# The row-maximum pass of a windowed attention in tiles of 32 queries x 4 heads by 160 keys

## What is computed

```python
mask = (j <= i) & (j >= i - 128)
q = (x @ Wq.T + bq).reshape(B, 512, 16, 8)    # k and v alike
scores = einsum('bqhd,bkhd->bhqk', q, k) / sqrt(8)
scores = where(mask, scores, -10000.0)
attn = softmax(scores, axis=-1) + 1e-9
ctx = einsum('bhqk,bkhd->bqhd', attn, v).reshape(B, 512, 128)
return ctx @ Wo.T + bo
```

## Time and profile before

| | us |
|---|---|
| median of 3 runs | 1092.84 (1092.12 to 1097.75) |
| the profiled execution's span | 1090.0 |
| TensorE busy in it | 783.8 (72%) |
| VectorE | 704.6 (65%) |
| GpSimd | 573.2 (53%) |
| ScalarE | 410.4 (38%) |

### The profile page before, as it was taken

The page is one execution under the profiler, slowest core; times in us unless marked ns, Lnnn a source line. Parts: engine busy times, 40 slices in busy tenths (PEclk is TensorE's granted clock), DMA queues, the critical chain, the costliest instruction groups (busy, mean ns, idle before and its releaser), DMA issues.

```text
span 1090.0 us, 21702 instructions
## 1 busy us (share of the span) xinstructions
PE 783.8 (72%) x6716; PEld 547.0 (50%) x6716; DVE 704.6 (65%) x2608; ACT 410.4 (38%) x690; POOL 573.2 (53%) x633
## 2 busy tenths in 40 slices
PE   4811887886677879788897979877777666666671
PEld 3611676665555525445454544445346555455560
DVE  7687778753545597675768667586857953445444
ACT  1360254443332415353434434354425433333330
POOL 5591562756545014463646443366447666666661
PEclk9999957998888959896989898896556898889886
DMA  8110012232223201010111101001002111222214
GB/s 233 26 29 10 21 41 60 57 60 62 57 65 79 71 22 50 21 53 23 48 47 29 51 12 49 3 3 30 11 15 61 38 45 45 62 74 82 69 40 128
DMA packets 62750, 54.05 MB, mean 50 GB/s; under 512 B 9986, under 2 KB 55812, under 8 KB 62636
## 3 DMA queue, kind: packets, MB, share of 16 engines
q1 hardware_dynamic: 53108, 33.12, 10.4%
q0 software_dynamic: 9536, 19.55, 7.1%
...
## 4 chain that ended last, share of the span: by engine, by line
PE 41%; DVE 28%; issue 10%; another core or an unknown queue 5%; ACT 5%; DVEq 4%; POOL 4%; DMA 3%; SPq 0%; POOLq 0%; ACTq 0%
PE stbank L1124 6%; DVE sbank L838 4%; PE stbank L1111 3%; PE sbank L1182 3%; PE bank L1211 3%; DVE zr L597 3%; PE stbank L1113 3%; PE stbank L1196 3%; PE stbank L1125 2%; DVE gl L778 2%; PE stbank L1112 2%; DVE xs L794 2%; ACT pT L966 2%; PE bank L1245 2%
## 5 line engine op out<-in xcount | busy, mean ns | idle before, releaser
L475 POOL DMA_INDIRECT xg<-table,idx x156 | 159.0, 1019 | 139.6 <-PE sbank L1092 63.4
L917 ACT ACTIVATE g<-stbank 128x512 f32<-128x512 f32 x156 | 93.3, 598 | 326.2 <-PE stbank L1113 247.6
L1124 PE MATMUL stbank<-wff,gh 128*128 x624 | 141.2, 305 | 100.1 <-DVE ysb L768 59.1
L838 DVE CUSTOM_DVE_ANT_0 sbank<-sbank,mband 128x256 f32<-128x256 f32 x384 | 152.2, 454 | 40.4 <-PE sbank L1182 29.9
L541 POOL TENSOR_SCALAR_AFFINE_SELECT pT<-pT 128x512 f32<-128x512 f32 x128 | 82.0, 641 | 177.3 <-ACT pT L966 177.0
L1111 PE MATMUL stbank<-xT,wff 128*128 128x128 f16 x624 | 151.2, 248 | 18.9 <-issue 11.1
L966 ACT ACTIVATE pT<-stbank 128x1024 f32<-128x1024 f32 (+1 forms) x128 | 116.9, 914 | 125.5 <-PE stbank L1196 124.6
L768 DVE TENSOR_REDUCE ysb<-stbank 128x128 f32<-128x256 f32 x156 | 65.9, 422 | 151.4 <-remote 90.1
L1113 PE MATMUL stbank<-xT,wff 128*128 128x128 f16 x624 | 151.5, 248 | 0.0
L1112 PE MATMUL stbank<-xT,wff 128*128 128x128 f16 x624 | 148.8, 244 | 0.0
L1124 PEld LDWEIGHTS stbank<-wff,gh 128*128 128x128 f16 x624 | 67.0, 107 | 132.5 <-issue 114.2
...
...
## 6 DMA issues: line engine op xcount, KB each, us to landing
...
qz<-dumps SPq DMA_DIRECT2D x96, 32.0 KB
kst<-dumps SPq DMA_DIRECT2D x96, 32.0 KB
xg<-table,idx POOLq DMA_INDIRECT x156
...
```

The costliest lines, as they stand in the source:

```text
L475: g.indirect_dma_start(xg[:, i % G].rearrange("p a d -> p (a d)"), None, table[cc % 2], bass.IndirectOffsetOnAxis(ap=idx[:, cc % 2, t:t + ...
L838: ins = v.tensor_tensor_reduce(out=src, in0=src, in1=m[:], scale=1.0, scalar=-3e38, op0=ALU.add, op1=ALU.max, accum_out=mx[:, qt, 4 * s + ...
L1124: mm(o, gh[:, i % 3, P * f:P * f + P], whl, start=(f == 0), stop=False, skip_group_check=True)
```

## The change

The maximum pass is tiled in another way. The queries of a block are numbered 32 n + q, with n = 0 to 3. One matmul takes the 32 queries of one n for all four heads of the set (4 x 32 = 128 rows) against the 160 keys that they can see. Two such make a half unit (`QW` = 32, `KW` = 160). Only the first and the last 32 of the 160 keys need a mask, the same triangles for every n: a third matmul adds them, `head4` (four identities side by side) times `corners`. In the first block, keys before the sequence's start are filled by small matmuls against `masked`, and each half unit has five matmuls. VectorE then takes one plain maximum over 2 x 160 per half unit.

To let one matmul pick the queries of one n of all heads, `qz` is laid out as (set and block, head, q, n), n fastest, so the weights are read with a step of four elements. With it change: the order of features in Wq and Wk (`head_order`), the write order of `hi`, `lo` (four instructions each) and `mT`, the pieces in which the stacks are read back, the affine selects' patterns on GpSimd, whose columns are now (q, n), and the transposes of `cx`, which become fp32 matmuls with a permutation (`unorder`) that puts the queries back in order.

```diff
@@ -32,6 +32,8 @@
+QW = 32
+KW = P + QW
@@ -98,7 +100,8 @@
-        mband = sb("mband", [P, 256], F16); mlower = sb("mlower", [P, P], F16)
+        head4 = sb("head4", [P, 4, QW], F16); corners = sb("corners", [P, 2, QW], F16); masked = sb("masked", [P, 1], F16)
+        unorder = sb("unorder", [P, 4, QW])
@@ -132,6 +135,8 @@
+        qv = qz[:].rearrange("p u (s t) (g n) -> p u s t g n", s=SETS, g=4)
@@ -176,6 +181,10 @@
+        def ordered(a, i):
+            a = a[:, i, :]
+            return a.rearrange("p (t q n) -> p t n q", q=QW, n=4) if i == 0 else a.rearrange("p (t n q) -> p t n q", n=4, q=QW)
@@ -336,10 +345,12 @@
                 for m in (2 * (k - 2), 2 * (k - 2) + 1):
                     i, g, c = m // 12, m // 3 % 4, m % 3
                     part = ((0, 0, 1), (0, 1, 0))[i][c]
-                    src = dumps[par, 2 * i + part].rearrange("(g s j) n -> g j s n", g=4, s=SETS)[g]
+                    src = dumps[par, 2 * i + part].rearrange("(g j s) n -> g j (s n)", g=4, s=SETS)[g]
...
-                    dst = (qz[r:r + DK, slot].rearrange("p (s g) n -> p s g n", g=4)[:, :, g, :] if i == 0 else kst[r:r + DK, slot, :, :])
-                    sp.dma_start(dst, src).then_inc(s_stk[par], 16)
+                    if i == 0:
+                        sp.dma_start(qz[r:r + DK, slot, :, P * g:P * g + P], src.rearrange("j (r n) -> j r n", n=P)).then_inc(s_stk[par], 16)
+                    else:
+                        sp.dma_start(kst[r:r + DK, slot].rearrange("j s n -> j (s n)"), src).then_inc(s_stk[par], 16)
@@ -517,15 +530,16 @@
-            made(g.affine_select(out=mband[:], in_=mband[:], compare_op=ALU.is_ge, fill=MASKED, base=0,
-                                 pattern=[[1, 256]], channel_multiplier=-1))
-            made(g.affine_select(out=mlower[:], in_=mlower[:], compare_op=ALU.is_ge, fill=MASKED, base=0,
-                                 pattern=[[-1, P]], channel_multiplier=1))
+            made(g.affine_select(out=head4[0:QW], in_=head4[0:QW], compare_op=ALU.not_equal, fill=1.0, base=0,
+                                 pattern=[[0, 4], [1, QW]], channel_multiplier=-1))
+            made(g.affine_select(out=corners[0:QW, 0, :], in_=corners[0:QW, 0, :], compare_op=ALU.is_ge, fill=MASKED, base=0,
+                                 pattern=[[1, QW]], channel_multiplier=-1))
+            made(g.affine_select(out=corners[0:QW, 1, :], in_=corners[0:QW, 1, :], compare_op=ALU.is_ge, fill=MASKED, base=0,
+                                 pattern=[[-1, QW]], channel_multiplier=1))
+            made(g.affine_select(out=unorder[:], in_=unorder[:], compare_op=ALU.not_equal, fill=1.0, base=0,
+                                 pattern=[[-1, 4], [-4, QW]], channel_multiplier=1))
...
-            pool.wait_ge(s_chain, made_n[0])
-            made(g.affine_select(out=mband[:], in_=mband[:], compare_op=ALU.is_ge, fill=MASKED, base=P,
-                                 pattern=[[-1, 256]], channel_multiplier=1))
@@ -538,11 +552,13 @@
                 i = UNITS * b + j
                 pool.wait_ge(s_e, i + 1)
                 p = pT[:, i % 3, 0:4 * w].rearrange("p (h q) -> p h q", q=w)
-                ins = g.affine_select(out=p[:, :, 0:P], in_=p[:, :, 0:P], compare_op=ALU.is_ge, fill=0.0, base=0,
-                                      pattern=[[0, 4], [1, P]], channel_multiplier=-1)
+                near = p[:, :, 0:P].rearrange("p h (q n) -> p h q n", n=4)
+                ins = g.affine_select(out=near, in_=near, compare_op=ALU.is_ge, fill=0.0, base=0,
+                                      pattern=[[0, 4], [1, QW], [QW, 4]], channel_multiplier=-1)
...
-                    ins = g.affine_select(out=p[:, :, P:256], in_=p[:, :, P:256], compare_op=ALU.is_ge, fill=0.0, base=0,
-                                          pattern=[[0, 4], [-1, P]], channel_multiplier=1)
+                    far = p[:, :, P:256].rearrange("p h (q n) -> p h q n", n=4)
+                    ins = g.affine_select(out=far, in_=far, compare_op=ALU.is_ge, fill=0.0, base=0,
+                                          pattern=[[0, 4], [-1, QW], [-QW, 4]], channel_multiplier=1)
@@ -811,8 +827,11 @@
                     i, bias = (0, bq_s) if j == 6 else (1, bk_s)
...
-                    v.scalar_tensor_tensor(out=lo[:, i, :], in0=bank[1][:, :], scalar=bias[:, 0:1], in1=hi[:, i, :],
-                                           op0=ALU.add, op1=ALU.subtract).then_inc(s_lo, 1)
+                    for t in range(TPB):
+                        ins = v.scalar_tensor_tensor(out=ordered(lo, i)[:, t], scalar=bias[:, 0:1], in1=ordered(hi, i)[:, t],
+                                                     in0=bank[1][:, P * t:P * t + P].rearrange("p (n q) -> p n q", n=4),
+                                                     op0=ALU.add, op1=ALU.subtract)
+                    ins.then_inc(s_lo, 1)
@@ -827,17 +846,13 @@
-                w = 256 if qt else 128
-                m = mband if qt else mlower
...
-                    for g in range(2 * half, 2 * half + 2):
-                        src = sbank[:, half, w * (g % 2):w * (g % 2) + w]
-                        ins = v.tensor_tensor_reduce(out=src, in0=src, in1=m[:], scale=1.0, scalar=-3e38, op0=ALU.add,
-                                                     op1=ALU.max, accum_out=mx[:, qt, 4 * s + g:4 * s + g + 1])
-                    ins.then_inc(s_red, 1)
+                    v.tensor_reduce(mx[:, 2 * half:2 * half + 2, TPB * s + qt],
+                                    sbank[:, half, 0:2 * KW].rearrange("p (n k) -> p n k", k=KW), AX.X,
+                                    ALU.max).then_inc(s_red, 1)
@@ -935,7 +950,8 @@
-                    a.activation(hi[:, i, :], bank[1][:, :], ACT.Identity, bias=bias[:, 0:1]).then_inc(s_hi, 1)
+                    a.activation(ordered(hi, i), bank[1][:, :].rearrange("p (t n q) -> p t n q", n=4, q=QW), ACT.Identity,
+                                 bias=bias[:, 0:1]).then_inc(s_hi, 1)
@@ -978,7 +994,8 @@
-                a.activation(mT[0:n], bank[1][0:n, :], ACT.Copy, scale=-1.0).then_inc(s_mt, 1)
+                a.activation(mT[0:n].rearrange("a (m n) -> a n m", n=4), bank[1][0:n, :].rearrange("a (n m) -> a n m", n=4),
+                             ACT.Copy, scale=-1.0).then_inc(s_mt, 1)
@@ -1176,12 +1193,24 @@
                     pe.wait_ge(s_stk[b % 2], 16 * 24 * (b // 2 + 1))
...
-                w = 256 if qt else 128
-                k0 = P * (qt - 1) if qt else 0
-                for g in range(2 * half, 2 * half + 2):
-                    ins = mm(sbank[:, half, w * (g % 2):w * (g % 2) + w], qz[0:P - 1, slot, 4 * s + g, P * qt:P * qt + P],
-                             kst[0:P - 1, slot, s, k0:k0 + w], start=True, stop=True)
-                ins.then_inc(s_s, 1)
+                heads = qz[0:P - 1, slot, TPB * s + qt, :]
+                for i in range(2):
+                    n = 2 * half + i
+                    q32 = heads[:, n:4 * P:4]
+                    o = sbank[:, half, KW * i:KW * i + KW]
+                    if qt:
+                        k0 = P * (qt - 1) + QW * n
+                        mm(o, q32, kst[0:P - 1, slot, s, k0:k0 + KW], start=True, stop=False, skip_group_check=True)
+                    else:
+                        w = QW * (n + 1)
+                        mm(o[:, 0:KW - w], head4[:], masked[:].to_broadcast([P, KW - w]), start=True, stop=False,
+                           skip_group_check=True)
+                        mm(o[:, KW - w:KW], q32, kst[0:P - 1, slot, s, 0:w], start=True, stop=False, skip_group_check=True)
+                o = sbank[:, half, 0:2 * KW].rearrange("p (n c k) -> p n c k", n=2, k=QW)
+                edges = slice(0 if qt else P // QW, KW // QW, P // QW)
+                m = corners[:] if qt else corners[:, 1:2, :]
+                mm(o[:, :, edges, :], head4[:], m.unsqueeze(1).to_broadcast([P, 2, m.shape[1], QW]), start=False, stop=True,
+                   skip_group_check=True).then_inc(s_s, 1)
@@ -1194,7 +1223,7 @@
                     ins = mm(bank_[:, w * g:w * g + w], kst[:, slot, s, P * kt:P * kt + P],
-                             qz[:, slot, 4 * s + g, P * kt:P * kt + w], start=True, stop=True)
+                             qv[:, slot, s, kt:kt + w // P, g, :], start=True, stop=True)
@@ -1236,7 +1265,7 @@
                     ins.then_inc(s_ut, 1)
...
-                    ins = pe.transpose(bank[0][:, P * qt:P * qt + P], cx[:, qt, :], ident[:])
+                    ins = mm(bank[0][:, P * qt:P * qt + P], cx[:, qt, :], unorder[:], start=True, stop=True)
@@ -1282,7 +1311,7 @@
 
...
-    return [DK * (SETS * s + g) + j for g in range(4) for s in range(SETS) for j in range(DK)]
+    return [DK * (SETS * s + g) + j for g in range(4) for j in range(DK) for s in range(SETS)]
```

6 lines of the change are left out of this document (4 added, 2 removed).

## The result

The changed kernel took **1241.99 us** in the median of 4 runs (1240.32 to 1246.96), beside 1094.53 us for the kernel before on the same chip (4 runs, 1092.12 to 1097.75): a ratio of **1.1346**, 95% interval 1.1308 to 1.1384. The profiled execution spans 1238.5 us, 148.5 more than before. The prediction was 1158, with 1218 as its upper end. The sign and the place were right, the size was not.

A forecast was written before the change was run, and what follows sets the result against it. No engine is full; a ring of waits through GpSimd's masks bounds the attention windows. Windows +64.9, de-ordering +4, first stage -3 make +66 us on 1092.8, rounded down to 1158 us; range 1112 to 1218.

The forecast's parts named there:

- the ring: Attention windows: product with V, scores, exponential, two masks, next product; 3.70 us for two units becomes 5.16.
- GpSimd's load: GpSimd's busy time in a window: 24 masks at 0.73 us more each add 17.5 us.
- the free-rows rival: GpSimd's masks: further pattern rows cost nothing, the maxima's gain stands, 1079 to 1085, say 1080 us; chance 0.09.
- The step that took 5.9 ns from `upto`: GpSimd's masks: each further pattern row costs 5.9 ns, so +0.73 us and a mask of 1.37 us.
- `prefer`'s 6.8 and `kst`'s 10.6: Other one-off GpSimd instructions' ns per further row; 6.8 gives 1171 us, 10.6 gives 1254 us, the latter's rival at 0.10.
- its own rule: Attention windows: each becomes the larger of ring and GpSimd's load, plus 2 us; +64.9 us in sum.
- would come on top: Attention windows: a granted clock falling to 1.2 GHz, since TensorE waits more, adds to the forecast; no size given.
- batch 7's ring: Last window, clock 0.54: the ring's TensorE part grows from 1.33 to 2.4 us, so 44 against 40.5, +3.5 us.
- the back parts: Beside a batch's back part: masks on units 0 and 1 cost 0, GpSimd being busy 4.49 of 17.21 us.
- +4 for the fp32 matmuls: De-ordering of cx by four fp32 matmuls instead of transposes: +0.5 us, 8 times; bounds +2 and +14.
- -3 for the first stage: First stage: cheaper maxima relieve VectorE, TensorE at a clock of 0.52 limits the gain; -3 us, bounds 0 and -7.
- the signs it named: Profile signs: masks 1.1 to 1.5 us, GpSimd over 730, VectorE below 660, first stage near 22, fp32 matmuls near 0.42.

The follow-up runs named there:

- the runs with 32, 64 and 128 rows: Kernel before, with only the masks' pattern split into 32, 64 or 128 rows for the same comparison: ratios 1.0221, 1.0704 and 1.1446.
- the run with long masks there alone: Kernel before, with the masks' pattern in rows of 4 in batch 7 alone, the other batches as before: ratio 1.0243.
- the repeated matmuls: Changed kernel, with query-key products of wide second half units in batches 1 to 7 made four times instead of once: ratio 1.1283, 1229.4 us.
- the kernel with free rows: Changed kernel with the masks' old pattern [0,4],[1,128], which clears wrong elements of the permuted columns: ratio 0.9917.

## Where the prediction was right and where it failed

Right: that the order of the queries would make the masks dear and that this would outweigh the maxima; the maxima's price and count (0.49 us forecast, 489 ns measured, 256 of them); the ring (5.64 by its rule, 5.67 in the trace at full clock); GpSimd's load (21.5 + 24 x 0.97 = 44.8 us in batches 1 to 3, 44.6 to 44.7 in the trace); that the maxima's gain is worth nothing behind a full GpSimd; the free-rows rival (1080, a ratio of 0.988; 0.9917 measured).

**Failed, the price of a row.** The step that took 5.9 ns from `upto` and left `prefer`'s 6.8 and `kst`'s 10.6 as bounds: measured 7.8. By its own rule with +0.97 a mask in place of +0.73: batch 0 (39.5 + 2) - 29.6 = +11.9; batches 1 to 3 (44.8 + 2) less 32.5, 32.0 and 32.0 = +43.9; batch 4 46.0 - 34.5 = +11.5; batch 5 41.5 - 29.1 = +12.4; batch 6 41.5 - 26.5 = +15.0; batch 7 some +6.9. Together +101.6 where it had +64.9: **37 us** of the miss. In batches 1 and 2 this is all: +14.3 and +14.8 by the rule, +14.2 and +14.7 measured. `upto` is one instruction of 64 elements, and 41 ns spread over seven rows is a thin base for 124; the runs with 32, 64 and 128 rows are what a price should rest on. The Trainium skill's rule (GPSIMD Engine Reference, section 3.1), by which rows would be free, does not agree with these runs.

**Failed, VectorE as an engine that GpSimd leaves alone.** No term of the sum had it. The text names VectorE's waits for other engines only, and costs its SBUF instructions at their old length. Batch 7: +18.8 instead of +3.5 (6.9 at the right row price), **12 us**, shown by the run with long masks there alone. Its part in batches 0 to 6 is not separated by a run. With masks of 1.6 us little of it lies in their windows: after the right row price and the clock (next), at most 1.9 us is left in any of them. It lies between them, where the chain has single instructions of 3.4 to 3.7 us.

**Failed, the clock as a remark.** The prediction said that a fall to 1.2 GHz "would come on top" and gave it no figure and no place in the range; only batch 7's ring was lengthened for it. The mean granted clock fell to 0.72 to 0.77 in batches 0 to 5 and to 0.60 in batch 6, which in the windows was worth **18 us**. It fits batch by batch: with the right row price the rule still misses +4.0, -0.1, -0.1, +4.1, +3.6, +4.5 and +4.5 us in batches 0 to 6, and the repeated matmuls took away 2.1, 0.3, 0.0, 4.4, 2.6, 5.3 and 3.6. In batch 6 the five rings alone, each 1.0 to 1.1 us longer than batch 5's, make 5.2. The prediction's own step for batch 7, the ring's TensorE part divided by the clock, would have priced it.

**Failed, the back parts.** "Beside the back part, where GpSimd is busy 4.49 of 17.21 us: 0" for the masks of units 0 and 1, +4 for the fp32 matmuls and -3 for the first stage: +1 outside the windows. Measured +14.6, **14 us** more. The seven stretches between windows grew by 4.8, -1.2, 4.2, 7.0, 1.2, 0.4 and 1.3, together 17.7; what lies ahead of the first window shrank by 0.3, what follows the last by 2.7. GpSimd itself leaves room there (8.24 of 24.25 us in the longest of them, from batch 3 to 4), so the zero was wrong for another reason. In that stretch the chain holds these two:

```profile
663.71 3.43 DVE rr L606
...
667.94 3.78 DVE zr L613 x2
```

After batch 0 it holds `zr` for 3.67 us and the output projection's matmuls at 0.72 each instead of 0.42. So both causes above are in it; how much each has isn't known. The first stage itself took 19.8 us where 22 were forecast, but it began 4.8 us later (384.1 against 379.3), so the first product with V came only 0.8 us sooner.

The four make 36.7 + 11.9 + 18.2 + 13.6 = 80.4 of the 82.6 us between the sum of 65.9 and the measured 148.5. They are not equally well founded: the first two are borne out by runs of whole kernels clear of noise, the clock's is a difference of two profiles that the whole kernel's time doesn't confirm, and the last is what was left outside the windows.

**Of the signs it named:** masks at 1.1 to 1.5 us (1.61), GpSimd over 730 us (789.7), VectorE's total below 660: it was 703.6, as before the change (704.6), although the maxima had fallen from 194 us (accumulator reads included, overlaps counted once) to 122. That total was the loudest sign that something else had been added. In the kernel with free rows it is 639.4. The de-ordering's four fp32 matmuls, two records of 370 ns each that overlap, take 1.7 us in the chain, 0.42 each as forecast. Writing `hi` and mT with a step, taken as 0, costs 0.73 us each time. The page's busy times of the changed kernel and of the one with free rows:

```profile
PE 854.7 (69%) x7132; PEld 603.5 (49%) x7132; DVE 703.6 (57%) x1888; ACT 428.6 (35%) x690; POOL 789.7 (64%) x636
```

```profile
PE 767.4 (75%) x7132; PEld 554.3 (54%) x7132; DVE 639.4 (62%) x1888; ACT 429.3 (42%) x690; POOL 575.2 (56%) x636
```
